# Four projection chunks of an attention layer: operations grouped into stages, PSUM banks dealt by purpose

## The chip, the cores and the metric

One core of a Trainium2 chip runs the whole program. The metric is the device time of one execution in microseconds. TensorE (PE) multiplies, ScalarE (ACT) and VectorE (DVE) work on what it leaves in PSUM, GpSimd (POOL) does small pieces, and SyncE (SP) issues most of the DMAs. PSUM has eight banks of 128 x 512 values in fp32, held here as one tensor `bank[:, 0..7, :]`.

## The reference, cut to what matters

The program computes five residual blocks over 2048 tokens of width 128: a dense mixture of experts, a state-space layer, the mixture again, a routed low-rank layer, an attention, and the low-rank layer again. The change touches the attention alone, between its normalization and its softmax:

```
q = x @ Wq; k = x @ Wk; v = x @ Wv
latent_kv = (k + v) @ W_down_kv            # 32 wide
k_rec = latent_kv @ W_up_k
v_rec = latent_kv @ W_up_v
scores = (q . k_rec) * scale               # 16 heads of 8, 2 batches of 1024
scores = clip(scores) * exp(-1e-4 * |i - j|); attn = softmax(scores)
out = (attn @ v_rec) @ Wo
```

## The kernel before, in words

The 2048 tokens are four chunks of 512 (NC = 4, CH = 512); chunks 0 and 1 are batch 0, chunks 2 and 3 are batch 1 (QC = 2). Each engine runs its own list of instructions in the order in which it was written, and semaphores tie the lists together. All that stands in `attn_rest` of each engine is the part that the change rewrites; what stands before it (the low-rank layer, ending with the normalization of chunk 3 at about 458 us) and behind it (`attn_bound`, `attn_spread`, `attn_fast`) keeps its code.

For one chunk c the projections are these steps, with the lines of the profile:

- PE `keys_values`: six matmuls of 128 x 512 (`split_matmul` twice, L1341 to L1343) add up k + v. ACT copies it to SBUF (L701, `kv_f`).
- PE `queries`: three such matmuls (L1341 to L1343). For chunks 0 and 1 DVE multiplies q with two position tables (`query_decay`, L1092, two instructions), ACT squares it (L709) and rounds the two products (`query_hi`, L717), and DVE takes the rests (`query_lo`, L1101). For chunks 2 and 3 DVE only copies q (`query_raw`, L1127), and ACT squares it.
- PE `latents`: one product with `w_down` (L1530). ACT copies it (L723, `lat_f`).
- PE `keys` (L1535) and `values_in` (L1540), both from `lat_f`. ACT squares the keys (L727) and copies the values out (`values_out`, L738). For chunks 0 and 1 DVE multiplies the keys with two tables (`key_decay`, L1107), ACT rounds (`key_hi`, L734), DVE takes the rests (`key_lo`, L1114). For chunks 2 and 3 DVE copies them (`key_raw`, L1131).
- PE `norms`: two products that sum the squares per head (L1551, L1552). DVE takes two maxima of them (`maxima`, L1121).

The rounded parts and rests go by DMA into four "stacks" (SP, L427), one per group of four heads; stack 0 of batch 0 is filled chunk by chunk, the others whole. The last `maxima` starts `attn_bound`: DVE, PE, DVE, POOL, PE and ACT in turn compute the bound that the softmax subtracts (L1179 to L1593, L794), and then the softmax's 256 exponentials run on ACT (L782) while PE computes scores (L1612) and weighted values (L1628).

Banks went by chunk: chunk c had four banks of its own, and chunk c + 2 had the same four:

```
return ((4, 5, 6, 7), (0, 1, 2, 3))[c % QC]   # q and its norms; k + v and then the values; latents and k norms; keys
```

The values of a chunk were written into the bank of k + v, so PE's `keys_values(c)` for c >= 2 waited for `v_copied`, that is for ACT's `values_out(c - 2)`.

Of the kernel before, what the change touches and what calls it, by code (L numbers as in the profile page):

```python
# [24 lines left out]
NC = T // CH  # L25
# [110 lines left out]
def build(nc, io):  # L136
    ctx = ExitStack()
    with ctx:
# [226 lines left out]
        def attn_banks(c):  # L365


            return ((4, 5, 6, 7), (0, 1, 2, 3))[c % QC]
# [9 lines left out]
        BOUND = attn_banks(QC)[3]  # L378
# [195 lines left out]
        def _(eng):  # L574
# [122 lines left out]
            def keys_values(c):  # L697
                eng.wait_ge(s["kv_ready"], c + 1)
                if c >= 2:
                    eng.wait_ge(s["lat_ready"], c - 1)  # L700
                eng.activation(kv_f(c), bank[:, attn_banks(c)[1], :], ACT.Copy).then_inc(s["kv_copied"], 1)  # L701

            def query_squares(c):
# [5 lines left out]
                eng.activation(squares(c)[0], bank[:, attn_banks(c)[0], :], ACT.Square, scale=SCALE)\  # L709
# [9 lines left out]
            def latents(c):  # L719
                eng.wait_ge(s["lat_ready"], c + 1)  # L720
                if c >= 2:
                    eng.wait_ge(s["v_ready"], c - 1)
                eng.activation(lat_f(c), bank[0:LAT, attn_banks(c)[2], :], ACT.Copy).then_inc(s["lat_copied"], 1)  # L723

            def key_squares(c):
                eng.wait_ge(s["k_ready"], c + 1)
                eng.activation(squares(c)[1], bank[:, attn_banks(c)[3], :], ACT.Square).then_inc(s["k_sq_ready"], 1)  # L727
# [8 lines left out]
            def values_out(c):  # L736
                eng.wait_ge(s["v_ready"], c + 1)
                eng.activation(values[c // QC][:, TPC * (c % QC):TPC * (c % QC + 1), :, 0:HD],  # L738
                               bank[:, attn_banks(c)[1], :].rearrange("p (t h d) -> p t h d", t=TPC, h=H), ACT.Copy)\
                   .then_inc(s["v_copied"], 1)  # L740

            def attn_first(c):
                keys_values(c)
                query_squares(c)
                query_hi(c)

            def attn_rest():
                attn_first(0)
                latents(0)
                keys_values(1)  # L750
                key_squares(0)
                key_hi(0)
                query_squares(1)
                query_hi(1)
                values_out(0)
                latents(1)
                keys_values(2)
                key_squares(1)
                key_hi(1)
                values_out(1)  # L760
                query_squares(2)
                latents(2)
                keys_values(3)
                key_squares(2)
                values_out(2)
                query_squares(3)
                latents(3)
                key_squares(3)
                values_out(3)
# [21 lines left out]
            def attention():  # L791
                attn_rest()
# [59 lines left out]
        def _(eng):  # L852
# [234 lines left out]
            def query_decay(c):  # L1087
                eng.wait_ge(s["q_ready"], c + 1)
                if c == 0:
                    eng.wait_ge(s["prep_loaded"], 16 * len(LATER))  # L1090
                for i in range(2):
                    eng.scalar_tensor_tensor(out=q_f[:, i, :], in0=bank[:, attn_banks(c)[0], :], scalar=SCALE,  # L1092
# [11 lines left out]
            def key_decay(c):  # L1104
                eng.wait_ge(s["k_sq_ready"], c + 1)
                for i in range(2):
                    eng.tensor_tensor(k_f[:, i, :], bank[:, attn_banks(c)[3], :], grow[:, i, place(c)], ALU.mult)\  # L1107
# [9 lines left out]
            def maxima(c):  # L1117
                b = c // QC
                eng.wait_ge(s["norms_ready"], c + 1)
                for i in range(2):  # L1120
                    last = eng.reduce_max(head_max[:, b, i, c % QC:c % QC + 1], bank[:, attn_banks(c)[2 * i], :],  # L1121
# [3 lines left out]
            def query_raw(c):  # L1125
                eng.wait_ge(s["q_ready"], c + 1)
                eng.tensor_copy(raw_of(q_f, c), bank[:, attn_banks(c)[0], :]).then_inc(s["q_raw"], 1)  # L1127

            def key_raw(c):
                eng.wait_ge(s["k_sq_ready"], c + 1)  # L1130
                eng.tensor_copy(raw_of(k_f, c), bank[:, attn_banks(c)[3], :]).then_inc(s["k_raw"], 1)  # L1131

            def attn_rest():
                query_decay(0)
                query_lo(0)
                key_decay(0)
                key_lo(0)
                query_decay(1)
                query_lo(1)
                maxima(0)  # L1140
                key_decay(1)
                key_lo(1)
                query_raw(2)
                maxima(1)
                key_raw(2)
                query_raw(3)
                maxima(2)
                key_raw(3)
                maxima(3)
# [188 lines left out]
        def _(pe):  # L1338
# [168 lines left out]
            def keys_values(c):  # L1507
                at, out = chunk(c), bank[:, attn_banks(c)[1], :]
# [11 lines left out]
            def queries(c):  # L1520
                at = chunk(c)
                if c >= 2:
                    pe.wait_ge(s["maxes_ready"], c - 1)
                split_matmul(bank[:, attn_banks(c)[0], :], sq_hi[:, WQ, :], sq_lo[:, WQ, :], xn_hi[:, at], xn_lo[:, at],
                             True, True).then_inc(s["q_ready"], 1)

            def latents(c):
                pe.wait_ge(s["prep_loaded"], 16 * len(LATER))
                pe.wait_ge(s["kv_copied"], c + 1)
                pe.matmul(bank[0:LAT, attn_banks(c)[2], :], w_down[:], kv_f(c), start=True, stop=True)\  # L1530
                  .then_inc(s["lat_ready"], 1)

            def keys(c):
                pe.wait_ge(s["lat_copied"], c + 1)
                pe.matmul(bank[:, attn_banks(c)[3], :], w_up[:, 0, :], lat_f(c), start=True, stop=True)\  # L1535
                  .then_inc(s["k_ready"], 1)

            def values_in(c):
                for t in range(TPC):
                    last = pe.matmul(bank[:, attn_banks(c)[1], 128 * t:128 * (t + 1)],  # L1540
# [3 lines left out]
            def norms(c):  # L1544
                pe.wait_ge(s["q_sq_ready"], c + 1)
                pe.wait_ge(s["k_sq_ready"], c + 1)
                if c >= 2:
                    pe.wait_ge(s["q_raw"], c - 1)
# [249 lines left out]
```

## Time and profile before

| | us |
|---|---|
| median of 3 runs | 824.15 |
| lowest, highest | 819.81, 825.55 |
| the profiled execution | 822.77 |
| its span, first to last instruction | 821.0 |
| PE busy, ACT busy, DVE busy, POOL busy in it | 718.6, 568.1, 497.7, 261.4 |

The span is what the trace's clock counts, 1.8 us less than the profiled execution's own time. All positions below are microseconds from the span's start. A busy PE may be a slow one: PEclk is the granted share of TensorE's full clock, 1.00 for 2.4 GHz and 0.50 for 1.2 GHz.

### The profile page before, as it was taken

To read this page: it belongs to the slowest core of one execution; us is meant where nothing else is said; L and a number is where in the kernel's file an instruction comes from. 1 tells how busy PE (TensorE), PEld (TensorE's weight loads), DVE (VectorE), ACT (ScalarE), POOL (GpSimd) and SP (SyncE) were. 2 spreads that over 40 slices of the span, in tenths; PEclk is the share of its full clock that TensorE was granted. 3 is DMA by queue.
4 is the path that set the end of the run, shared out by engine and by line. 5 is a ranking of instruction groups with operands and counts; after the bars stand their busy time and mean duration, and the time that the engine had idled before them with its cause. 6 is when DMAs were issued, how large, how long until landed. Compare 5 with 4: busy or idle time off the path is not lost.

```text
span 821.0 us, 11243 instructions
## 1 busy us (share of the span) xinstructions
PE 718.6 (88%) x3736; PEld 429.3 (52%) x3736; DVE 497.7 (61%) x1268; ACT 568.1 (69%) x800; POOL 261.4 (32%) x289
## 2 busy tenths in 40 slices
PE   2889889899898999999686696999999999999587
PEld 2567667676676777878564352323323232233364
DVE  4789878789788888888566442244423232222464
ACT  4557675667777666555344446999999999999243
POOL 2286466665666554555412000021200000000020
PEclk9999999999999999999758776999999999999958
DMA  9100000000000000000000269100079400000001
GB/s 269 42 0 2 0 1 1 0 1 2 0 1 1 0 1 2 0 1 1 0 1 0 52 127 196 36 1 1 1 134 194 85 2 1 1 1 1 3 1 51
DMA packets 14989, 24.94 MB, mean 30 GB/s; under 512 B 2720, under 2 KB 11376, under 8 KB 13424
## 3 DMA queue, kind: packets, MB, share of 16 engines
q1 hardware_dynamic: 13776, 23.79, 13.2%
q8 instruction: 31, 0.51, 0.3%
q0 software_dynamic: 224, 0.34, 0.2%
q14 instruction: 30, 0.25, 0.1%
q10 hardware_dynamic: 928, 0.06, 0.1%
HBM read 6.35 MB, written 1.05 MB: 9 GB/s over the span
## 4 chain that ended last, share of the span: by engine, by line
ACT 28%; PE 14%; issue 9%; DVE 5%; POOL 4%; ACTq 0%; POOLq 0%; DVEq 0%
ACT raw_w L782 25%; POOL act_parts L539 3%; PE bank L1341 2%; PE bank L1342 2%; PE bank L1343 2%; PE bank L1628 1%; ACT xt L609 1%; PE bank L1381 1%; PE bank L1535 1%; PE bank L1396 1%; PE bank L1612 1%; DVE xn_parts L875 1%; PE bank L1397 1%; POOL rstd L488 1%; DVE stats L865 1%
## 5 line engine op out<-in xcount | busy, mean ns | idle before, releaser
L782 ACT ACTIVATE raw_w<-bank,minus_c 128x1024 f32<-128x1024 f32 x256 | 259.3, 1161 | 4.8 <-DVE bank L1221 2.6
L539 POOL TENSOR_TENSOR act_parts<-act,act_parts 128x512 fp32r<-128x512 f32 x128 | 168.5, 1318 | 151.1 <-ACT act_parts L671 148.2
L657 ACT ACTIVATE glu<-bank,b_gate 128x512 f32<-128x512 f32 x128 | 88.1, 688 | 113.5 <-PE bank L1343 112.8
L1221 DVE TENSOR_TENSOR bank<-bank,fix 128x256 f32<-128x256 f32 x128 | 55.3, 433 | 180.4 <-PE bank L1612 180.4
L1341 PE MATMUL bank<-xn_parts,w_hi 128*128 128x512 f32 x256 | 108.0, 422 | 15.7 <-DVE up L999 8.0
L1343 PE MATMUL bank<-xn_parts,w_hi 128*128 128x512 f32 x256 | 103.0, 402 | 0.0
L1342 PE MATMUL bank<-xn_parts,w_lo 128*128 128x512 f32 x256 | 102.4, 400 | 0.0
L999 DVE TENSOR_SCALAR up<-bank,b_up 128x512 f32<-128x512 f32 x113 | 84.2, 745 | 24.7 <-PE bank L1343 24.0
L1003 DVE SCALAR_TENSOR_TENSOR bank<-glu,bank 128x512 f32<-128x512 f32 x128 | 87.9, 687 | 7.3 <-ACT glu L657 7.1
L1012 DVE SCALAR_TENSOR_TENSOR act<-up,bank 128x512 f32<-128x512 f32 x128 | 87.9, 687 | 4.4
L671 ACT ACTIVATE act_parts<-act 128x512 fp32r<-128x512 f32 x128 | 80.1, 626 | 14.8 <-DVE act L1012 14.5
L485 POOL TENSOR_SCALAR var_eps<-mean_var 128x4 f32<-128x4 f32 x28 | 7.1, 254 | 237.8 <-DVE mean_var L869 236.5
L1628 PE MATMUL bank<-raw_w 128*9 128x512 f32 x512 | 68.7, 609 | 0.0
L1628 PE MATMUL bank<-raw_w,act 128*9 128x512 f32 x512 | 68.2, 595 | 0.0
L1341 PEld LDWEIGHTS bank<-xn_parts,w_hi 128*128 128x128 f32 x256 | 49.6, 194 | 32.5 <-DVE up L999 12.3
L1463 PE MATMUL bank<-act_parts,w_hi 128*128 128x512 f32 x128 | 53.0, 414 | 4.8 <-POOL act_parts L539 4.7
L1343 PEld LDWEIGHTS bank<-xn_parts,w_hi 128*128 128x128 f32 x256 | 49.2, 192 | 11.5
L1342 PEld LDWEIGHTS bank<-xn_parts,w_lo 128*128 128x128 f32 x256 | 49.7, 194 | 9.0
L1460 PE MATMUL bank<-act_parts,w_hi 128*128 128x512 f32 x128 | 52.0, 407 | 0.4 <-ACT act_parts L671 0.4
L1448 PE MATMUL bank<-score_t,sel 128*128 128x512 f32 x128 | 51.4, 402 | 0.0
L1461 PE MATMUL bank<-act_parts,w_lo 128*128 128x512 f32 x128 | 51.4, 401 | 0.0
L609 ACT ACTIVATE xt<-bank,offset,rstd 128x128 f32<-128x128 f32 x96 | 35.9, 457 | 17.8 <-POOL offset L494 17.8
(195 smaller groups left out, 1071.2 us busy)
## 6 DMA issues: line engine op xcount, KB each, us to landing
raw_w<-in_gate_up SPq DMA_DIRECT2D x4, 512.0 KB, 9.1
w_lo<-gelu_parts SPq DMA_DIRECT2D x8, 256.0 KB, 5.4
w_lo<-act_parts SPq DMA_DIRECT2D x8, 256.0 KB, 5.5
w_hi<-gelu_parts SPq DMA_DIRECT2D x6, 256.0 KB, 4.6
w_hi<-act_parts SPq DMA_DIRECT2D x6, 256.0 KB, 5.6
x_tok<-in_x SPq DMA_DIRECT2D x4, 256.0 KB, 4.4
raw_w<-in_down SPq DMA_DIRECT2D x4, 256.0 KB, 8.5
grow<-in_grow SPq DMA_DIRECT2D x1, 1024.0 KB, 7.4
```

Of the source, the lines that this page charges most:

```text
L539: pool.tensor_tensor(act_lo[:, j % NACT, :], act[:, j % NACT, :], act_hi[:, j % NACT, :].bitcast(F32), ALU.subtract).then_inc(s["lo_ready" ...
L657: eng.activation(glu[:, j % 2, :], bank[:, G, :], ACT.Gelu_apprx_sigmoid, bias=b_gate[:, e:e + 1]).then_inc(s["glu_ready"], 1)
L671: eng.activation(act_hi[:, j % NACT, :], act[:, j % NACT, :], ACT.Copy).then_inc(s["hi_ready"], 1)
L782: eng.activation(probs[:, u % NP, :], pair, ACT.Exp, bias=minus_c[:, b:b + 1])\
L999: eng.tensor_scalar(up[:, j % 2, :], bank[:, U, :], b_up1[:, e:e + 1], 1.0 - LIMIT, ALU.add, ALU.max).then_inc(s["up_ready"], 1)
L1003: eng.scalar_tensor_tensor(out=bank[:, S[j % 2], :], in0=glu[:, j % 2, :], scalar=GLU_AT_LIMIT, in1=bank[:, S[j % 2], :], op0=ALU.min, op1 ...
L1012: eng.scalar_tensor_tensor(out=act[:, j % NACT, :], in0=up[:, j % 2, :], scalar=1.0 + LIMIT, in1=bank[:, S[j % 2], :], op0=ALU.min, op1=AL ...
L1221: eng.tensor_tensor(pair, pair, turned, ALU.mult)\
L1341: pe.matmul(out, w_hi, v_hi, start=start, stop=False)
L1342: pe.matmul(out, w_lo, v_hi, start=False, stop=False)
L1343: return pe.matmul(out, w_hi, v_lo, start=False, stop=stop)
L1628: last = pe.matmul(bank[32 * j:32 * j + VW, 6 + n % 2, :], values[b][:, kb, HG * g + j, :], probs[:, u % NP, CH * (j % 2):CH * (j % 2 + 1) ...
```

## The change

The banks are dealt by purpose: two for q (and its norms), two for k + v, one for the latents, two for the keys (and their norms), one for the values. A new function orders the operations of every engine: at each step come `norms` of the chunk three back, `keys_values` of the newest, `latents` and `queries` of the one before, `keys` and `values_in` of the one before that. DVE waits for its own rests of the chunk before (`q_lo_ready`, `k_lo_ready`) before it overwrites `q_f` or `k_f`; `norms` now waits for the keys' decay or copy too.

```diff
-        def attn_banks(c):
-            return ((4, 5, 6, 7), (0, 1, 2, 3))[c % QC]
+        Q_BANK, KV_BANK, LAT_BANK, K_BANK, V_BANK = (0, 1), (4, 5), 3, (6, 7), 2
+        def projections(kv, latents_queries, keys_and_values, norms):
+            for step in range(NC + 3):
+                for op, stage in ((norms, 3), (kv, 0), (latents_queries, 1), (keys_and_values, 2)):
+                    if 0 <= step - stage < NC:
+                        op(step - stage)
...
 # ScalarE
+            def latents_queries(c):
+                latents(c)
                 query_squares(c)
-                query_hi(c)
+                if c < QC:
+                    query_hi(c)
+            def keys_and_values(c):
+                key_squares(c)
+                if c < QC:
+                    key_hi(c)
+                values_out(c)
...
-                attn_rest()
+                projections(keys_values, latents_queries, keys_and_values, lambda c: None)
...
 # VectorE
             def query_decay(c):
                 eng.wait_ge(s["q_ready"], c + 1)
+                if c >= 1:
+                    eng.wait_ge(s["q_lo_ready"], 2 * c)
...
             def key_decay(c):
                 eng.wait_ge(s["k_sq_ready"], c + 1)
+                if c >= 1:
+                    eng.wait_ge(s["k_lo_ready"], 2 * c)
...
+            def latents_queries(c):
+                if c < QC:
+                    query_decay(c)
+                    query_lo(c)
+                else:
+                    query_raw(c)
+            def keys_and_values(c):
+                if c < QC:
+                    key_decay(c)
+                    key_lo(c)
+                else:
+                    key_raw(c)
...
-                attn_rest()
+                projections(lambda c: None, latents_queries, keys_and_values, maxima)
...
 # TensorE
             def keys_values(c):
...
-                elif c == 1:
-                    pe.wait_ge(s["xn_ready"], nth_hi(LN_ATTN, NC - 1))
-                else:
-                    pe.wait_ge(s["v_copied"], c - 1)
+                elif c >= 2:
+                    pe.wait_ge(s["kv_copied"], c - 1)
...
             def latents(c):
-                pe.wait_ge(s["prep_loaded"], 16 * len(LATER))
+                if c == 0:
+                    pe.wait_ge(s["prep_loaded"], 16 * len(LATER))
+                else:
+                    pe.wait_ge(s["lat_copied"], c)
...
             def keys(c):
                 pe.wait_ge(s["lat_copied"], c + 1)
+                if c >= 2:
+                    pe.wait_ge(s["maxes_ready"], c - 1)
...
             def values_in(c):
+                if c >= 1:
+                    pe.wait_ge(s["v_copied"], c)
...
             def norms(c):
...
+                if c < QC:
+                    pe.wait_ge(s["q_decayed"], 2 * c + 2)
+                    pe.wait_ge(s["k_decayed"], 2 * c + 2)
                 else:
-                    pe.wait_ge(s["q_decayed"], 2 * c + 2)
+                    pe.wait_ge(s["q_raw"], c - QC + 1)
+                    pe.wait_ge(s["k_raw"], c - QC + 1)
...
-                attn_rest()
+                projections(keys_values, latents_queries, keys_and_values, norms)
```

VectorE, from the first decay of the queries on, before (glu_s are the decayed queries, up the decayed keys, head_max the maxima):

```order
L1092 SCALAR_TENSOR_TENSOR glu_s<-bank,grow 128x512 x2
L1101 TENSOR_TENSOR act_parts<-glu_s,gelu_parts 128x512 x2
L1107 TENSOR_TENSOR up<-bank,grow 128x512 x2
L1114 TENSOR_TENSOR xn_parts<-up,early 128x512 x2
L1092 SCALAR_TENSOR_TENSOR glu_s<-bank,grow 128x512 x2
L1101 TENSOR_TENSOR act_parts<-glu_s,gelu_parts 128x512 x2
L1121 TENSOR_REDUCE head_max<-bank 128x1 x2
L1107 TENSOR_TENSOR up<-bank,grow 128x512 x2
```

VectorE at the same place, now (the lines of the new file lie some ten lower):

```order
L1082 SCALAR_TENSOR_TENSOR glu_s<-bank,grow 128x512 x2
L1091 TENSOR_TENSOR act_parts<-glu_s,gelu_parts 128x512 x2
L1082 SCALAR_TENSOR_TENSOR glu_s<-bank,grow 128x512 x2
L1091 TENSOR_TENSOR act_parts<-glu_s,gelu_parts 128x512 x2
L1099 TENSOR_TENSOR up<-bank,grow 128x512 x2
L1106 TENSOR_TENSOR xn_parts<-up,early 128x512 x2
L1113 TENSOR_REDUCE head_max<-bank 128x1 x2
L1120 COPY glu_s<-bank 128x512
L1099 TENSOR_TENSOR up<-bank,grow 128x512 x2
```

The queries of chunk 1 have moved ahead of the keys of chunk 0, and so has everything that waits for VectorE's decay of those keys moved behind them.

TensorE, from the keys of chunk 0 to the keys of chunk 1, before (w_up are keys and values, w_down the latents, same_head the norms, three rows with sq_hi, sq_lo, sq_hi one product of q or half of one of k + v):

```order
L1535 MATMUL bank<-tmp,w_up 128x512
L1540 MATMUL bank<-w_up,tmp 128x128 x4
L1341 MATMUL bank<-xn_parts,sq_hi 128x512
L1342 MATMUL bank<-xn_parts,sq_lo 128x512
L1343 MATMUL bank<-xn_parts,sq_hi 128x512
L1530 MATMUL bank<-glu,w_down 32x512
L1551 MATMUL bank<-score_t,same_head 128x512
L1552 MATMUL bank<-score_t,same_head 128x512
L1341 MATMUL bank<-xn_parts,sq_hi 128x512
```

TensorE from the keys of chunk 0 on, now:

```order
L1530 MATMUL bank<-tmp,w_up 128x512
L1537 MATMUL bank<-w_up,tmp 128x128 x4
L1550 MATMUL bank<-score_t,same_head 128x512
L1551 MATMUL bank<-score_t,same_head 128x512
L1331 MATMUL bank<-xn_parts,sq_hi 128x512
L1332 MATMUL bank<-xn_parts,sq_lo 128x512
```

The queries and latents of chunk 1 have gone to the front of this piece, with k + v of chunk 2 ahead of them; the norms of chunk 0 come straight behind the values of chunk 0, and k + v of chunk 3 behind the norms.

## Rows read from the trace of the kernel before

**Rows 1.** Stretches of the span: busy us of each engine (instructions), granted clock, DMA.

```profile
core 0: us, PE busy (x) PEld busy (x) DVE busy (x) ACT busy (x) POOL busy (x), PEclk, DMA share, GB/s
...
456.30:498.55 42.25, 32.53 (x98) 18.04 (x97) 20.22 (x36) 16.44 (x30) 0.71 (x1) 0.74 0.55 116
498.55:772.00 273.45, 256.91 (x1813) 84.08 (x1814) 84.20 (x200) 261.69 (x260) 11.93 (x8) 0.98 0.23 45
```

**Rows 2.** The chain of waits at the end of the projections: start us, us, what.

```profile
492.87 1.30 DVE head_max L1121 x2
...
498.55 0.85 PE bank L1612 x3
```

**Rows 3.** The same view of stretches, the projections cut where the granted clock changes.

```profile
456.30:460.40 4.10, 4.10 (x11) 2.78 (x9) 1.02 (x3) 1.19 (x2) 0.00 (x0) 0.50 0.00 0
460.40:470.64 10.24, 7.20 (x26) 3.44 (x25) 6.37 (x10) 4.79 (x9) 0.00 (x0) 1.00 0.35 82
470.64:484.30 13.66, 11.85 (x26) 6.79 (x27) 6.30 (x11) 6.22 (x12) 0.00 (x0) 0.50 0.44 101
484.30:494.20 9.90, 8.22 (x34) 4.44 (x32) 5.32 (x10) 4.06 (x7) 0.00 (x0) 1.00 0.97 177
...
498.55:508.20 9.65, 8.19 (x44) 2.67 (x48) 1.63 (x4) 7.03 (x7) 0.00 (x0) 0.50 0.98 190
```

**Rows 4.** Timeline around TensorE's gap: start us, us, engine, line, operation.

```profile
472.45 0.76 PE L1341 MATMUL bank<-xn_parts,sq_hi 128*128 128x512 f32 x1 [3.90 <-ACT raw_w L738]
```

**Rows 5.** Timeline, TensorE at 2.4 GHz.

```profile
462.43 0.39 PE L1342 MATMUL bank<-xn_parts,sq_lo 128*128 128x512 f32 x1
462.66 0.40 PE L1343 MATMUL bank<-xn_parts,sq_hi 128*128 128x512 f32 x1
464.01 1.12 PE L1535 MATMUL bank<-tmp,w_up 32*128 32x512 f32 x2 [0.95 <-ACT tmp L723]
464.97 1.05 PE L1540 MATMUL bank<-w_up,tmp 32*128 32x128 f32 x8
...
465.95 0.51 PE L1341 MATMUL bank<-xn_parts,sq_hi 128*128 128x512 f32 x1
...
466.85 1.04 PE L1530 MATMUL bank<-glu,w_down 128*32 128x512 f32 x2
467.83 0.50 PE L1551 MATMUL bank<-score_t,same_head 128*128 128x512 f32 x1
```

**Rows 6.** Timeline, TensorE at 1.2 GHz.

```profile
459.44 0.63 PE L1342 MATMUL bank<-xn_parts,sq_lo 128*128 128x512 f32 x1
...
459.86 0.63 PE L1343 MATMUL bank<-xn_parts,sq_hi 128*128 128x512 f32 x1
...
475.28 2.07 PE L1535 MATMUL bank<-tmp,w_up 32*128 32x512 f32 x2
...
477.15 1.91 PE L1540 MATMUL bank<-w_up,tmp 32*128 32x128 f32 x8
478.99 0.80 PE L1341 MATMUL bank<-xn_parts,sq_hi 128*128 128x512 f32 x1
...
480.57 1.92 PE L1530 MATMUL bank<-glu,w_down 128*32 128x512 f32 x2
```

**Rows 7.** Timeline, the first queries between VectorE and ScalarE.

```profile
460.53 1.29 DVE L1092 SCALAR_TENSOR_TENSOR glu_s<-bank,grow 128x512 f32<-128x512 f32 x2 [2.04 <-PE bank L1343]
...
461.85 0.60 ACT L709 ACTIVATE score_t<-bank 128x512 fp32r<-128x512 f32 x1 [2.01 <-DVE glu_s L1092]
...
462.34 1.14 ACT L717 ACTIVATE gelu_parts<-glu_s 128x512 fp32r<-128x512 f32 x2
...
463.07 1.29 DVE L1101 TENSOR_TENSOR act_parts<-glu_s,gelu_parts 128x512 fp32r<-128x512 f32 x2 [1.25 <-ACT gelu_parts L717]
```

**Rows 8.** Timeline, SyncE's issue of the last rests of stack 0.

```profile
481.30 1.26 SPq L427 DMA_DIRECT2D w_hi<-xn_parts  x2
```

**Rows 9.** The page of DMA issues, 440 to 620: issues, KB each, median us to landing.

```profile
w_hi<-xn_parts SPq DMA_DIRECT2D x4, 128.0 KB, 2.6
```

More of the change, by code:

```diff
@@ L376, in out_bank @@
             return 4 + c
-        BOUND = attn_banks(QC)[3]
+        BOUND = K_BANK[1]
         UNITS = G4 * QC * KB * 2
@@ L700, in keys_values @@
                     eng.wait_ge(s["lat_ready"], c - 1)
-                eng.activation(kv_f(c), bank[:, attn_banks(c)[1], :], ACT.Copy).then_inc(s["kv_copied"], 1)
+                eng.activation(kv_f(c), bank[:, KV_BANK[c % 2], :], ACT.Copy).then_inc(s["kv_copied"], 1)
             def query_squares(c):
@@ L708, in query_squares @@
                     eng.wait_ge(s["q_decayed"], 2 * c + 2)
-                eng.activation(squares(c)[0], bank[:, attn_banks(c)[0], :], ACT.Square, scale=SCALE)\
+                eng.activation(squares(c)[0], bank[:, Q_BANK[c % 2], :], ACT.Square, scale=SCALE)\
                    .then_inc(s["q_sq_ready"], 1)
@@ L722, in latents @@
                     eng.wait_ge(s["v_ready"], c - 1)
[L723 removed]
+                eng.activation(lat_f(c), bank[0:LAT, LAT_BANK, :], ACT.Copy).then_inc(s["lat_copied"], 1)
             def key_squares(c):
                 eng.wait_ge(s["k_ready"], c + 1)
[L727 removed]
+                eng.activation(squares(c)[1], bank[:, K_BANK[c % 2], :], ACT.Square).then_inc(s["k_sq_ready"], 1)
             def key_hi(c):
@@ L738, in values_out @@
                 eng.activation(values[c // QC][:, TPC * (c % QC):TPC * (c % QC + 1), :, 0:HD],
-                               bank[:, attn_banks(c)[1], :].rearrange("p (t h d) -> p t h d", t=TPC, h=H), ACT.Copy)\
+                               bank[:, V_BANK, :].rearrange("p (t h d) -> p t h d", t=TPC, h=H), ACT.Copy)\
                    .then_inc(s["v_copied"], 1)
-            def attn_first(c):
-                keys_values(c)
+            def latents_queries(c):
+                latents(c)
                 query_squares(c)
-                query_hi(c)
[L747 to L769, printed above, removed]
+                if c < QC:
[5 more added lines that the diff above has]
+                values_out(c)
             def attn_fast():
@@ L1091, in query_decay @@
                 for i in range(2):
-                    eng.scalar_tensor_tensor(out=q_f[:, i, :], in0=bank[:, attn_banks(c)[0], :], scalar=SCALE,
+                    eng.scalar_tensor_tensor(out=q_f[:, i, :], in0=bank[:, Q_BANK[c % 2], :], scalar=SCALE,
                                              in1=grow[:, 1 - i, place(c)], op0=ALU.mult, op1=ALU.mult)\
@@ L1120, in maxima @@
                 for i in range(2):
-                    last = eng.reduce_max(head_max[:, b, i, c % QC:c % QC + 1], bank[:, attn_banks(c)[2 * i], :],
+                    last = eng.reduce_max(head_max[:, b, i, c % QC:c % QC + 1], bank[:, (Q_BANK, K_BANK)[i][c % 2], :],
                                           axis=AX.X)
@@ L1507, in keys_values @@
             def keys_values(c):
-                at, out = chunk(c), bank[:, attn_banks(c)[1], :]
+                at, out = chunk(c), bank[:, KV_BANK[c % 2], :]
                 pe.wait_ge(s["xn_ready"], nth_hi(LN_ATTN, c))
@@ L1534, in keys @@
                 pe.wait_ge(s["lat_copied"], c + 1)
-                pe.matmul(bank[:, attn_banks(c)[3], :], w_up[:, 0, :], lat_f(c), start=True, stop=True)\
+                if c >= 2:
+                    pe.wait_ge(s["maxes_ready"], c - 1)
+                pe.matmul(bank[:, K_BANK[c % 2], :], w_up[:, 0, :], lat_f(c), start=True, stop=True)\
                   .then_inc(s["k_ready"], 1)
             def values_in(c):
+                if c >= 1:
+                    pe.wait_ge(s["v_copied"], c)
                 for t in range(TPC):
-                    last = pe.matmul(bank[:, attn_banks(c)[1], 128 * t:128 * (t + 1)],
+                    last = pe.matmul(bank[:, V_BANK, 128 * t:128 * (t + 1)],
                                      lat_f(c)[:, 128 * t:128 * (t + 1)], w_up[:, 1, :], start=True, stop=True)
```

70 lines of the change are left out of this document (18 added, 52 removed).

## The prediction

> **What bounds the kernel now.** I read three views in this order: the stretches of the span, the chain of waits behind the projections, and the timeline of the projections. The stretches [rows 1] set the ceiling: the projections take 456.30 to 498.55, 42.25 us of 821.0, and behind them ACT is busy 261.69 of 273.45 us with the exponentials. So the softmax is bound by ACT, and whatever the projections end earlier or later moves its start, and with it the end of the program, one for one. Ahead of 456.30 nothing is touched. What sets the end of the projections is the last pair of maxima on DVE, 492.87 to 494.16, and from there a serial chain through five engines runs to 498.55, 5.68 us after the pair's start [rows 2]. That chain keeps its code and its cost. The question is only when the last maxima start.
>
> Cut where the granted clock changes [rows 3], PE is busy 4.10 of 4.10, 7.20 of 10.24, 11.85 of 13.66 and 8.22 of 9.90 us: at 1.2 GHz it is nearly full and is the bound, at 2.4 GHz it waits for the others. The one large hole is 3.90 us before k + v of chunk 2 at 472.45, released by the copy of chunk 0's values on ACT (L738, `values_out`) [rows 4]. That is the bank wait that the change takes away. After this hole the clock was at 1.2 GHz from 470.64 to 484.30, so the hole costs more than its own length.
>
> **The prices of a step.** At 2.4 GHz a 128x512 matmul follows the one before after 0.23 us and its result is there 0.40 after its start; keys take 0.96, values 0.98, latents 0.98, and the q product with its restart 0.90, without a wait 0.70 [rows 5]. At 1.2 GHz the step is 0.43 (result after 0.63), keys 1.87, values 1.84, latents 1.85 (estimated like them, since it issues as many columns at 2.4 GHz in 0.98 as values do), q 1.28 without a wait and 1.58 with its restart [rows 6]. Norms are two steps with a restart, about 0.7 and 1.1 (estimated from the steps). On DVE a pair takes 1.29; ACT's square is 0.60 and lets the next start after 0.49; the rounding pair takes 1.14, and DVE's rests start 0.73 after ACT's first rounding [rows 7]. A handover costs 0.03 to 0.04 (460.49, when q was there, to 460.53) [rows 6, 7].
>
> **What the change removes, adds and moves, walked through with the clock as traced** (1.2 GHz to 460.4, 2.4 to 470.6, 1.2 to 484.3, 2.4 behind). No instruction is added or removed; all the work of the engines stays.
>
> Chunk 1's k + v now goes ahead of the queries: it runs 458.87 to 461.05, latents of chunk 0 to 462.02, queries of chunk 0 are ready at 462.89. Before they were ready at 460.49 [rows 6]: DVE's chain starts 2.4 us later. PE goes on with k + v of chunk 2 (462.72), latents and queries of chunk 1, keys and values of chunk 0, without a hole to 467.7: the removed wait does go away here. Then come the norms of chunk 0, which now also wait for the keys' decay. On DVE that decay stands behind both chunks' queries: decay of q0 462.92 to 464.22, ACT's square and first rounding to 465.34, rests to 466.67; decay of q1 466.69 to 468.00 (queued behind its new wait for the rests, about 0.1 each), ACT to 469.12, rests to 470.44; decay of k0 to 471.67. Two rounds of 1.30 + 1.14 + 1.30 and a pair of 1.30 stand between q0 and the norms. The norms start at 471.69, so PE is idle 3.98 us where it was idle 3.90: the hole keeps its place and length and gets another cause. Queued behind these norms on PE are k + v of chunk 3, latents and queries of chunk 2 and the keys of chunk 1, so everybody waits.
>
> From there PE is at 1.2 GHz and full: norms to 472.81, k + v 3 to 475.38, latents 2 to 477.23, queries 2 to 478.52, keys 1 to 480.38, values 1 to 482.2. Norms 1 wait for the decay of k1, 482.54, a hole of 0.35, and run 482.57 to 483.69. Latents 3 run to 485.2, queries 3 wait for the maxima of chunk 1 and run 485.24 to 486.04, keys 2 to 487.00, values 2 to 487.98; norms 2 wait for the copy of k2, 488.80 (a hole of 0.82), keys 3 489.48, values 3 to 491.4, norms 3 wait for the copy of k3, 491.98 (0.56), and end at 492.79. The last maxima run 492.82 to 494.11.
>
> The same bookkeeping with the old order ends at 493.47 (the trace has 494.16, so it is 0.7 us short). Like against like the new order is 0.6 us later, and the 4.4 us behind it stay.
>
> **The unknown: which clock goes with the new order.** Where a span falls at which level is not in my hands, so I bound it by running both orders at the same levels. At 2.4 GHz from 460.4 on: new 490.2, old 488.3, +1.9. At 1.2 GHz throughout: 501.6 against 500.6, +1.0. At 1.2 GHz from 470.6 on: 497.8 against 499.0, -1.3. The order alone is thus worth -1.3 to +1.9. The clock itself can differ between the two: against the traced level of before (493.5), the new order ends at 490.2 if the hole doesn't cost the clock, -3.2, and at 497.8 if the clock doesn't come back at 484, +4.3. In the new order the last third has more holes on PE (0.35, 0.14, 0.82, 0.56), so the upper side is likelier. I take +2.0, nearest to the row of equal clocks (+0.6) with less than half of the way to +4.3.
>
> On such holes the rows show: a gap of 0.95 us ahead of the keys of chunk 0 at 464.01 [rows 5] left the clock at 2.4 GHz, the gap of 3.90 us did not [rows 3, 4]. The Trainium skill, page "TensorE: Matmul & The Clock Gate", section "A second HAM failure mode: psum-queue depth-cycling", speaks against this change: a kernel that goes round PSUM banks leaves TensorE so many small idle spots between groups of matmuls that its clock swings between the two levels. By that rule the last third here would go at 1.2 GHz; by the row of the 0.95 us gap it would not. It is rival two below.
>
> **Covers.** SP fills stack 0 when the rests of k1 are there: before it issued them at 481.30 [rows 8]; now they come at 483.9, and with 1.26 for the two issues [rows 8] and 2.6 to landing [rows 9] they are in by some 488, over 10 us ahead of 498.55. So the later rests cost nothing; without that cover they would cost the 2.6 us. Stacks 1 to 3 shift by the same 2.6 us, and the first is read only after a quarter of batch 0's 128 exponentials. ACT has 16.44 us of work in 42.25 [rows 1], so its new order hides. DVE's two new waits for its own rests cost 0.1 each and are in the walk. PE's new waits for `lat_copied`, `v_copied` and `maxes_ready` end before PE is there, except queries 3 (0.14).
>
> **The sum.** Profiled execution 822.8 + 2.0 = 824.8. It lies 1.4 below the median of the three runs; against that the sum would be 826.2. I forecast 825.5, between the two. A measurement of this kernel tells about 1% (8.2 us) from no change, and this is far below.
>
> **The rivals.**
>
> One, the forecast: the hole stays, with the keys' decay as its cause; 823 to 826.5. Chance 0.50.
>
> Two, the clock is lost in the last third too: 822.8 + 4.3 = 827.1. For it: more small holes, work of chunk 3 spread thin. Against it: the old order had holes there too (8.22 busy of 9.90 [rows 3]) and kept 2.4 GHz. Chance 0.20.
>
> Three, the pipeline does what it is built for: PE's hole is short enough, or falls such that the clock stays at 2.4 GHz from 460.4 on: 822.8 - 3.2 = 819.6. For it: PE has five operations queued over the first part of DVE's work. Against: DVE's chain from q0 to the norms is 8.8 us, PE's queue behind q0 5.0 us, and that leaves four. Chance 0.12.
>
> Four, on the slower side: the clock never rises to 2.4 GHz at 460.4. The place is PE between k + v of chunk 1 and the norms of chunk 0; once at 1.2 GHz the whole stretch is bound by PE and ends at 501.6, +8.1, and the softmax's start at 1.2 GHz, where ACT was busy 7.03 of 9.65 us [rows 3] against 96% later [rows 1], costs some 2.2 us more if it lasts as long again: 833.1. It decides from a granted clock of 0.5 between 461 and 470. Against it: PE is as full there as before (no hole from 456.3 to 467.7). Chance 0.08.
>
> Five, the change moves nothing at the start of the softmax, since orders and waits offset each other (the -1.3 to +0.6 of equal clocks): 822.8, as before. Chance 0.10.
>
> **How the numbers follow.** The likeliest is one, 825.5. The range reaches from case three (819.6) to above case two, and leaves out most of four: 819.5 to 830. Over 1% faster only with a clock better than anywhere traced, 0.03; over 1% slower is case four, 0.08; the rest, 0.89, is within 1%.
>
> **What would show it right or wrong.** Right: the norms of chunk 0 start within 0.1 us of the end of the keys' decay of chunk 0 and after a PE gap of 3 to 5 us; k + v of chunk 2 run without a wait at about 463; the last maxima start 1 to 4 us later than 492.87, counted from k + v of chunk 0; the 5.68 us from them to the first scores unchanged. Wrong: a PE gap under 2 us before the norms of chunk 0 (then three), a first score held by a stack rather than by the bound, or a change of more than 2 us anywhere ahead of 456 or behind 499.

## The result, and the profile after

The changed kernel runs in 823.76 us (median of 20 runs, 820.91 to 829.39); the kernel before, run beside it, in 821.5 (20 runs, 815.68 to 825.92). The ratio on record is 1.0045 with a 95% interval of 1.0025 to 1.0066: some 3.7 us slower, a small loss that is clear of no change and within 1%. It is not the quotient of the two medians, which lie 2.3 us apart (1.0028, inside the interval). The profiled execution has a span of 823.4 us against 821.0.

First the stretches of the changed kernel's trace, cut where its granted clock changes (columns as in [rows 1]). The fifth row is the last third of the projections, the last two are the whole projections and the softmax:

```profile
453.88:459.20 5.32, 5.32 (x14) 3.79 (x12) 1.02 (x3) 1.19 (x2) 0.00 (x0) 0.50 0.01 3
459.20:469.45 10.25, 7.21 (x27) 3.70 (x26) 5.66 (x9) 5.88 (x11) 0.00 (x0) 1.00 0.22 52
469.45:476.28 6.83, 5.99 (x11) 3.13 (x12) 3.19 (x6) 2.61 (x5) 0.00 (x0) 0.50 0.48 116
476.28:479.70 3.42, 2.63 (x13) 1.55 (x12) 1.48 (x3) 1.39 (x4) 0.00 (x0) 1.00 0.29 75
479.70:496.00 16.30, 14.33 (x31) 7.40 (x31) 7.64 (x12) 5.26 (x9) 0.00 (x0) 0.50 0.81 153
...
453.88:500.81 46.93, 36.65 (x98) 20.17 (x97) 20.21 (x36) 16.50 (x30) 0.72 (x1) 0.65 0.52 110
500.81:774.20 273.39, 257.10 (x1814) 84.08 (x1814) 84.30 (x200) 261.68 (x260) 11.92 (x8) 0.98 0.22 44
```

The projections take 46.93 us, k + v of chunk 0 to the first scores, where they took 42.25; the softmax behind them is as long as it was (273.39 against 273.45 us, ACT busy 261.68 against 261.69) [rows 1]. TensorE's work is the same in matmuls, but its busy time rose from 32.53 to 36.65, since more of it ran at 1.2 GHz: the mean clock of the stretch is 0.65 instead of 0.74.

The timeline shows where TensorE waited and when the last maxima came. The first number in brackets is how long the engine had been idle before the row, and behind the arrow stands what released it; such idle time of TensorE is called a **hole** below:

```profile
453.88 0.78 PE L1331 MATMUL bank<-xn_parts,sq_hi 128*128 128x512 f32 x1
...
461.06 0.39 PE L1331 MATMUL bank<-xn_parts,sq_hi 128*128 128x512 f32 x1
...
468.87 1.28 DVE L1099 TENSOR_TENSOR up<-bank,grow 128x512 f32<-128x512 f32 x2
...
470.29 0.77 PE L1550 MATMUL bank<-score_t,same_head 128*128 128x512 f32 x1 [3.88 <-DVE up L1099]
...
480.35 0.77 PE L1550 MATMUL bank<-score_t,same_head 128*128 128x512 f32 x1 [1.43 <-DVE up L1099]
...
494.72 1.29 DVE L1113 TENSOR_REDUCE head_max<-bank 128x1 f32<-128x512 f32 x2 [1.54 <-PE bank L1551]
...
500.81 1.22 PE L1593 MATMUL bank<-w_hi 32*128 32x512 f32 x6 [1.89 <-issue]
```

The row at 461.06 is k + v of chunk 2, without a wait: the bank wait that held it for 3.90 us [rows 4] is gone. The row at 470.29 has taken its place: the norms of chunk 0 wait 3.88 us for the keys' decay (L1099, the old L1107), which DVE starts at 468.87 behind both chunks' queries. Norms of chunk 1 wait 1.43 us for the same operation of chunk 1.

From here on **stretch** means the time from the first matmul of k + v of chunk 0 to the start of the last pair of maxima: 492.87 - 456.30 = 36.57 us before, 494.72 - 453.88 = 40.84 after, +4.27. (Where DVE's maxima of two chunks run together, I count back 1.32 us from the operation behind them, as in before's 494.19 - 492.87.) The bound's chain behind it took 6.09 instead of 5.68 us. Against these +4.7 stands that k + v of chunk 0 started 2.42 us earlier, in code that the change doesn't touch. -2.42 + 4.27 + 0.41 and some 0.1 of rest make the 2.4 us between the spans.

Where in the stretch the 4.27 us arise, a cut at the norms of chunk 1 shows. They start 482.41 - 456.30 = 26.11 us behind k + v of chunk 0 in the trace of before and 480.35 - 453.88 = 26.47 us in the changed kernel's: up to there the two are level, holes of 3.90 and 3.88 us included, though the changed kernel has done k + v of chunk 3 by then (at a mean granted clock of 0.76 against 0.70). From there to the last maxima, before and then after:

```profile
482.41:492.87 10.46, 10.11 (x38) 5.96 (x37) 4.66 (x8) 4.64 (x8) 0.00 (x0) 0.91 0.98 184
```

```profile
480.35:494.72 14.37, 14.33 (x31) 7.37 (x31) 5.86 (x10) 4.61 (x8) 0.00 (x0) 0.50 0.84 160
```

So 3.91 of the 4.27 us lie behind the norms of chunk 1. The changed kernel has seven matmuls fewer left there, but does them all at 1.2 GHz, TensorE busy for 14.33 of 14.37 us, where before had a granted clock of 0.91. The level fell at 479.70, in the hole of 1.43 us ahead of the norms of chunk 1, which the old order doesn't have. These are two single executions. For every execution the mean granted clock of the whole span is on record: its median is 0.927 over the 20 runs of the changed kernel and 0.931 over the 35 runs of before that stand beside the first experiments.

### The profile page after: what moved, and what is told of

The parts are those of the page before. It is cut to its first block, busy times and chain, and to the rows that moved or that the text cites. A ratio compares the mean times of both kernels' runs of the same rounds, so it can differ in the third digit from the quotient of the medians.

```text
span 823.4 us, 11254 instructions
## 1 busy us (share of the span) xinstructions
PE 722.0 (88%) x3736; PEld 430.4 (52%) x3736; DVE 497.3 (60%) x1268; ACT 568.2 (69%) x800; POOL 261.3 (32%) x289
## 4 chain that ended last, share of the span: by engine, by line
ACT 27%; PE 15%; issue 9%; DVE 5%; POOL 4%; ACTq 0%; POOLq 0%; DVEq 0%
ACT raw_w L770 25%; POOL act_parts L544 3%; PE bank L1331 2%; PE bank L1333 2%; PE bank L1332 2%; PE bank L1609 1%; ACT xt L614 1%; PE bank L1371 1%; PE bank L1386 1%; PE bank L1387 1%; PE bank L1593 1%; PE bank L1523 1%; DVE xn_parts L863 1%; POOL rstd L493 1%; DVE stats L853 0%
```

## The experiments

All ratios are against the kernel before, run on the same chip, with the 95% interval. Next to the time stands the stretch of each run's one trace. The trace is one execution and its clock levels vary: in these kernels, the same ahead of the projections, k + v of chunk 0 started anywhere from 452.99 to 459.67 us. So the time's interval decides and the stretch explains. In the filled kernel before, below, the traced execution took 823.34 us with a stretch of only 31.6, and the median of its runs was 817.74.

The kernel before had a median of 821.9 us (35 runs) beside the first comparison of the banks alone, the keys ahead of queries in the first and third form, and the changed kernel filled; 819.91 (29 runs) beside the second form, before filled, the first comparison of the decays first and the second of the banks alone; and 821.59 (16 runs) beside the rest. The quotient of the medians lies inside the interval each time, but not always near the ratio; gains in microseconds go by the ratio where the medians are not named.

**The banks alone (two comparisons).** The new banks with their waits, but `projections` replaced on all three engines by the old lists (on ACT with `attn_first` written out):

```diff
-                projections(keys_values, latents_queries, keys_and_values, norms)
+                keys_values(0)
+                queries(0)
+                latents(0)
+                keys_values(1)
+                keys(0)
+                values_in(0)
...
+                norms(3)
```

Expected:

> The new banks and their waits with the old order on all three engines. Stretch means: from the first matmul of k + v of chunk 0 to the start of the last pair of maxima, 36.6 us in the trace of before and 40.8 in that of the changed kernel. Theory A (the loss is the new order: on VectorE the queries of chunk 1 stand ahead of the keys' decay of chunk 0, for which the norms of chunk 0 wait): the hole of 3.9 us before k + v of chunk 2 closes, the stretch is 33 to 36 us, and the time 1 to 3 us below before. Rival B (the loss is the dealing of the banks with its waits between TensorE and the others): stretch 38 to 41, time 1 to 3 us above before. Rival C (only the clock's levels fell otherwise, by chance): stretch 36 to 38, no difference.

> The new banks with the old order once more, since its first comparison was 0.9957 to 1.0015 and its trace had a stretch of 30.8 us. Theory A: stretch 30 to 35 and a time 1 to 4 us below before; taken together with the first, clear of no change. If the banks alone are worth nothing: ratio 1.000 within 0.2%.

Measured: 818.42 us, ratio 0.9986 (0.9957 to 1.0015), stretch 30.7; then 817.61, ratio 0.9967 (0.9935 to 0.9999), stretch 33.7. Both stretches are shorter than before's 36.57, and theory A's direction holds, though only the second interval stays, barely, below 1 (in the first the medians lie 3.5 us apart, the ratio says 1.1). The holes don't close as expected: before the keys of chunk 1 TensorE waits 1.34 us in the first trace and 2.88 us in the second, for ACT's copy of the latents (L728), and behind the 2.88 the clock falls to 0.50 for 6.83 us. What is clear is the comparison with the changed kernel: its 1.0025 to 1.0066 doesn't overlap either. With the new banks the old order costs nothing, the new order does. The rival that blamed the banks, and the one that saw chance alone, fall. The order alone on the old banks can't be tried: it puts k + v of chunk 2 ahead of the values of chunk 0, and with the old banks that would wait for them forever. So banks and order aren't fully parted: the norms wait for the keys' decay only since the new banks put the keys' norms into the keys' bank (before they went into the latents' bank), and the order makes that wait long. The new order with the norms of the keys in a bank of their own was not run.

**Keys ahead of queries, in three forms.** First on all engines:

```diff
-                for op, stage in ((norms, 3), (kv, 0), (latents_queries, 1), (keys_and_values, 2)):
+                for op, stage in ((norms, 3), (kv, 0), (keys_and_values, 2), (latents_queries, 1)):
```

> The changed kernel with keys_and_values ahead of latents_queries within a step, on all engines. Theory A: the keys of chunk 0 are decayed ahead of the queries of chunk 1, the norms of chunk 0 start without a hole of 3.9 us, the stretch is 33 to 36 us, the time 1 to 3 us below before (4 to 6 below the changed kernel). Rival B (banks and their waits): stretch 39 to 41 as in the changed kernel. Rival C (chance): the stretch keeps a hole of about 4 us and ends between 36 and 41.

Measured: 822.54 us, ratio 1.0012 (0.9986 to 1.0038), stretch 33.3. The hole before the norms of chunk 0 is down to 0.24 us, but others appear later, the largest of them 1.67 us (timeline, TensorE):

```profile
470.81 0.47 PE L1550 MATMUL bank<-score_t,same_head 128*128 128x512 f32 x1 [0.24 <-DVE up L1099]
...
477.47 0.79 PE L1331 MATMUL bank<-xn_parts,sq_hi 128*128 128x512 f32 x1 [1.67 <-DVE head_max L1113]
```

The queries of chunk 2 now wait for maxima that stand behind other work on DVE. The stretch and the closed hole are as theory A has them; the gain is about half of what I wrote (2.7 us from the changed kernel's ratio to this one's, with overlapping intervals, not 4 to 6, and nothing measurable against before, where I had written 1 to 3).

Then with `keys_and_values` first of all:

```diff
+                for op, stage in ((keys_and_values, 2), (norms, 3), (kv, 0), (latents_queries, 1)):
```

> The changed kernel with keys_and_values first in a step, then norms, keys_values, latents_queries. Theory A: the stretch is 31 to 35 us, since TensorE's norms of chunk 0 find the keys' decay done; time 1 to 4 us below before. Rival B (banks and their waits cost): 38 to 41.

Measured: 819.5 us, ratio 0.9991 (0.9962 to 1.002), stretch 32.4. Its interval lies below the changed kernel's, but a gain over before (I had written 1 to 4 us) is not shown.

Last with TensorE's order left as changed, and only ACT and DVE taking the keys first, by a flag that their two calls set:

```diff
+                ops = [(norms, 3), (kv, 0), (latents_queries, 1), (keys_and_values, 2)]
+                if late_queries:
+                    ops = [ops[0], ops[1], ops[3], ops[2]]
+                for op, stage in ops:
```

> As the changed kernel on TensorE, but ScalarE and VectorE take keys_and_values ahead of latents_queries. Theory A with VectorE's list alone as the cause: the hole before the norms of chunk 0 shrinks to under 1 us, and the stretch is near 37. If TensorE's list matters too (the keys of chunk 0 still stand behind the queries of chunk 1, and the rests of the queries now wait behind them): hole gone but new ones ahead of the queries' consumers, stretch 38 to 40, time 0 to 2 us below the changed kernel. Rival B: no change, 40 to 41.

Measured: 824.71 us, ratio 1.0039 (1.0009 to 1.007), stretch 37.5. The hole shrinks from 3.88 to 1.21 us, and a new one of 2.08 us comes up before the queries of chunk 2:

```profile
468.22 0.48 PE L1553 MATMUL bank<-score_t,same_head 128*128 128x512 f32 x1 [1.21 <-DVE up L1102]
...
474.88 0.50 PE L1334 MATMUL bank<-xn_parts,sq_hi 128*128 128x512 f32 x1 [2.08 <-DVE head_max L1116]
```

The stretch lies between the two that I had written, near 37 for ACT's and DVE's lists alone and 38 to 40 if TensorE's matters too. So these two lists alone aren't enough; the lists have to fit each other. The time is not measurably below the changed kernel's.

**The holes filled.** What a hole costs by itself and what by the clock behind it: 16 matmuls, whose result nobody reads, go into it. In the changed kernel:

```diff
             def norms(c):
+                if c == 0:
+                    for _ in range(16):
+                        pe.matmul(bank[:, KV_BANK[1], :], sq_hi[:, WK, :], xn_hi[:, chunk(3)], start=True, stop=True)
```

> The changed kernel with 16 extra matmuls of 128x512 (their result is never read) on TensorE ahead of the norms of chunk 0, where it was idle for 3.9 us: 16 x 0.23 = 3.7 us at 2.4 GHz. Theory A says that the hole costs mainly the clock: the level stays at 2.4 GHz behind it, the stretch falls from 40.8 to 33 to 35 us, the time by 4 to 7 us although work was added. If the hole's cost is its own length and the queue order alone, the stretch stays at 40 to 41 and the time at that of the changed kernel or above.

In the kernel before:

```diff
             def keys_values(c):
                 at, out = chunk(c), bank[:, attn_banks(c)[1], :]
+                if c == 2:
+                    for _ in range(16):
+                        pe.matmul(bank[:, attn_banks(1)[1], :], sq_hi[:, WK, :], xn_hi[:, chunk(3)], start=True, stop=True)
```

> The kernel before with the same 16 extra matmuls on TensorE ahead of k + v of chunk 2, where it was idle for 3.9 us. If the hole costs the clock (theory A's second half): the stretch falls from 36.6 to 31 to 33 us, at 2.4 GHz throughout, and is 2 us shorter than in the filled changed kernel (35.0), which is what the order alone costs. If the levels have nothing to do with the hole: 36 to 37.

Measured: the changed kernel filled 821.3 us, ratio 1.001 (0.9975 to 1.0044), stretch 35.0; before filled 817.74, ratio 0.997 (0.9934 to 1.0005), stretch 31.6. Timeline of TensorE in the filled changed kernel:

```profile
466.36 3.96 PE L1544 MATMUL bank<-xn_parts,sq_hi 128*128 128x512 f32 x16
470.32 0.47 PE L1553 MATMUL bank<-score_t,same_head 128*128 128x512 f32 x1
...
470.86 0.39 PE L1331 MATMUL bank<-xn_parts,sq_hi 128*128 128x512 f32 x1
...
477.65 0.47 PE L1553 MATMUL bank<-score_t,same_head 128*128 128x512 f32 x1 [1.43 <-DVE up L1099]
...
478.43 1.92 PE L1523 MATMUL bank<-glu,w_down 128*32 128x512 f32 x2
```

The norms of chunk 0 now run at 2.4 GHz, and k + v of chunk 3 behind them takes 0.23 us a step where it took 0.43. The stretch fell by 5.8 us though 16 matmuls were added, but not all of that is the filling: in this trace the clock rose to 1.00 already 2.3 us behind the start of k + v of chunk 0, in the unfilled one 5.3 us behind it, and the norms start 15.00 us behind it instead of 16.41. From the norms of chunk 0 to the last maxima it is 20.03 instead of 24.43 us, 4.4 less: that is what the clock behind the hole costs here. In the kernel before the part ahead of the hole is level: k + v of chunk 2 starts 16.16 us behind k + v of chunk 0 (16.15 unfilled), and from there the last maxima come after 15.48 instead of 20.42 us, 4.9 less. The level then falls around the hole of 1.43 us before the norms of chunk 1 (latents 1.92 for two at 478.43), the same hole at which the unfilled kernel lost it. The time of the changed kernel fell by less than I wrote (2.9 us by the ratios, and the intervals overlap), and for before filled the interval just includes no change. With both holes of 3.9 us filled the new order stays 3.4 us of stretch behind the old one, where I had written 2: so this hole is not what sets the two orders apart. The filled changed kernel still lost the clock twice (0.50 from 478.05 to 481.46 and from 484.87 on), the filled before kept 1.00 from 464.68 to 491.98.

**The decays first: a version that beats both.** The new banks, with lists written by hand. DVE decays queries and keys of a chunk before it takes the rests of either:

```diff
 # VectorE
-                projections(lambda c: None, latents_queries, keys_and_values, maxima)
+                query_decay(0)
+                key_decay(0)
+                query_lo(0)
+                query_decay(1)
+                key_lo(0)
+                key_decay(1)
+                maxima(0)
+                key_lo(1)
+                query_lo(1)
+                query_raw(2)
+                maxima(1)
+                key_raw(2)
+                query_raw(3)
+                key_raw(3)
+                maxima(2)
+                maxima(3)
```

TensorE's list, in short names (kv, lat for latents, q, k, v, norm, with the chunk): kv0 kv1 lat0 q0 k0 v0 q1 lat1 kv2 k1 norm0 v1 kv3 lat2 q2 norm1 k2 v2 lat3 q3 k3 norm2 v3 norm3. ScalarE's (ks, qs the squares, kh, qh the roundings, vo the values out): kv0 lat0 kv1 ks0 qh0 qs0 vo0 lat1 kh0 ks1 qh1 kv2 kh1 qs1 lat2 vo1 kv3 ks2 qs2 vo2 lat3 ks3 qs3 vo3.

> The new banks with lists written by hand: VectorE decays queries and keys of a chunk before it takes the rests of either (decay q0, decay k0, rests q0, decay q1, rests k0, decay k1, maxima 0, rests k1, rests q1), so ScalarE's rounding is never waited for, and TensorE has the norms of chunk 0 behind the keys of chunk 1. Theory A in full (what counts is how early VectorE's decays free TensorE): no hole over 1.5 us on TensorE, clock at 2.4 GHz from some 460 to 490, stretch 25 to 29 us, time 5 to 9 us below before. If TensorE's own work at the granted clock is the bound instead: stretch not under 31.

> The hand-written lists with the new banks once more (the first comparison was 0.985 to 0.993, its trace had a stretch of 25.4 us). If that is the kernel and not the luck of its runs: stretch 25 to 29 us, ratio 0.987 to 0.993.

Measured: 812.04 us, ratio 0.9887 (0.9847 to 0.9927), stretch 25.4; again 814.27, ratio 0.9883 (0.984 to 0.9925), stretch 26.2. The stretches are as expected. The time is 9.3 and 9.6 us less by the ratios, 7.9 and 7.3 by the medians, against the 5 to 9 that I had written. The second run's stretches of two microseconds, the first and the last of those from the middle of the projections to their end (those between have TensorE busy 2.00 each, at 1.00):

```profile
462.00:464.00 2.00, 2.00 (x12) 1.38 (x11) 1.61 (x3) 1.17 (x3) 0.00 (x0) 1.00 0.00 0
...
480.00:482.00 2.00, 1.16 (x7) 0.60 (x5) 2.00 (x5) 0.60 (x1) 0.00 (x0) 1.00 0.95 184
```

TensorE is busy without a hole, at 2.4 GHz, to the end. Against the kernel before that is 10 to 11 us less stretch and 7 to 10 us less time. All three engines' lists changed at once, so these runs don't say which of the moves matters.

**The same lists on the old banks.** The kernel before, with the lists of the decays first as far as its banks let them, and DVE's new waits for its own rests. TensorE: kv0 q0 lat0 kv1 k0 v0 q1 lat1 kv2 k1 norm0 v1 kv3 q2 lat2 norm1 k2 v2 q3 lat3 k3 norm2 v3 norm3; ScalarE: kv0 lat0 kv1 ks0 qs0 vo0 qh0 lat1 kh0 ks1 qh1 kv2 kh1 vo1 qs1 kv3 lat2 qs2 ks2 vo2 qs3 lat3 ks3 vo3; VectorE as above.

```diff
             def query_decay(c):
                 eng.wait_ge(s["q_ready"], c + 1)
+                if c >= 1:
+                    eng.wait_ge(s["q_lo_ready"], 2 * c)
...
```

> The same lists on the old banks (chunk by chunk), as far as these let them: queries ahead of latents on TensorE, ScalarE's copies of the values earlier, since k + v of chunk 2 waits for the copy of chunk 0's values and k + v of chunk 3 for that of chunk 1's. If the order of VectorE's list is nearly all of the gain (theory A): stretch 26 to 30 us, time 4 to 8 us below before. If the gain needs the new banks: stretch 31 to 36, time 0 to 4 below before.

Measured: 818.51 us, ratio 0.9947 (0.9917 to 0.9976), stretch 31.0. The old wait is back:

```profile
473.70 0.47 PE L1349 MATMUL bank<-xn_parts,sq_hi 128*128 128x512 f32 x1 [2.08 <-ACT raw_w L738]
```

So reordering on the old banks gives about half of the gain, and the new banks with the lists that go with them the other half: the stretches differ by 4.7 us and the ratios by 0.6%, though the intervals still overlap by a little (0.9917 against 0.9925). The split isn't clean, since TensorE's and ScalarE's lists are not the same in the two (here the queries go ahead of the latents and of k + v of chunk 1). Theory A's claim that the order is nearly all of it is not borne out.

**The clock for the softmax's start.** On top of the decays first: 7, 5 and 6 unread matmuls where TensorE idles in the bound's chain.

```diff
             def attn_bound():
+                for _ in range(7):
+                    pe.matmul(bank[:, KV_BANK[0], :], sq_hi[:, WK, :], xn_hi[:, chunk(3)], start=True, stop=True)
                 pe.wait_ge(s["tops_ready"], 1)
...
```

> The hand-written lists with the new banks, and extra matmuls of 128x512 (never read) where TensorE idles behind the projections: 7 ahead of the wait for the maxima, 5 ahead of the wait for the bound, 6 behind it. The first 9.65 us of the softmax ran at 1.2 GHz in before, with ScalarE busy 7.03. If the idle spots of the bound's chain cost the clock there: the granted clock is 1.00 at the softmax's start, its first 10 us have ScalarE busy over 8.5, and the time is 1 to 3 us below the same kernel without them. If the extra matmuls only stand in the way of the chain: the chain grows by their overhang, up to 1 us, and the time is the same or 1 us more.

Measured: 811.34 us, ratio 0.9845 (0.9804 to 0.9885), the lowest ratio of all, but its interval overlaps that of the kernel without the extra matmuls (0.984 to 0.9925). The first 9.65 us of the softmax, with them and without:

```profile
489.95:499.60 9.65, 7.84 (x46) 2.35 (x48) 1.91 (x5) 7.33 (x7) 0.00 (x0) 0.65 0.93 195
```

```profile
487.96:497.61 9.65, 8.19 (x48) 2.46 (x48) 1.95 (x5) 7.08 (x7) 0.00 (x0) 0.55 1.00 200
```

The clock was at 1.00 when the scores started and fell to 0.50 2.4 us later: ACT is busy 7.33 instead of 7.08, not the 8.5 that I had written. The bound's chain did not grow: 5.8 us from the last maxima to the first scores, against 6.4 and 6.7 in the two traces without. A gain in time is not shown.

## Why the prediction was right, point by point

- **The frame held.** The softmax's start moves the end one for one; nothing behind it changed (273.39 against 273.45 us), and 16.5 us of ACT work hid in the new order.
- **The removed wait and its successor held.** k + v of chunk 2 without a wait (461.06, 7.2 us behind k + v of chunk 0, forecast 6.4); the norms of chunk 0 released by the keys' decay after 3.88 us, forecast 3.98, and 0.14 us behind its end, where I had written within 0.1. The norms of chunk 1 come 26.47 us behind k + v of chunk 0, forecast 482.57 - 456.30 = 26.27. That the holes are equally long also means that this exchange is not the loss: the loss comes behind it. The banks alone show that it takes the new order.
- **The sum held, the walk in the last third did not.** Forecast was +2.0 against the profiled execution; the 20 runs say +3.7 (2 to 5.4) by the ratio and +2.3 by the medians. The forecast's walk takes 492.82 - 482.57 = 10.25 us from the norms of chunk 1 to the last maxima, with the clock back at 2.4 GHz at 484.3. The trace takes 14.37, since the level falls at 479.70 and stays at 1.2 GHz to the end. I had allowed for that by less than half of the way to +4.3, the price of rival two (the clock lost in the last third).
- **Rival two had the level right and not the reason.** Its "more small holes" (0.14, 0.82 and 0.56 us behind the norms of chunk 1) are not there: at 1.2 GHz TensorE was full. Its walk was at 1.2 GHz from 470.6 on, while the trace had 3.42 us at 2.4 GHz from 476.28. That the stretch grew by 4.27, so near to 4.3, is in part luck. By the time of the 20 runs the forecast's own case (823 to 826.5) came true, and the traced execution, 825.18 us at a mean clock of 0.923, is among the lower clocks of the 20 (0.921 to 0.934). How many of them lost the clock in the last third is not on record.
- **The absolute level** came out 1.7 us under mine. I had set 825.5 between the profiled execution's 822.8 + 2.0 and the median's 824.15 + 2.0, and the runs of before beside it had a median of 821.5.
- **The signs that I named.** The last maxima came 4.3 us later in the stretch, outside my 1 to 4. The chain behind them grew by 0.4, not 0, all in TensorE's wait that the profile puts down to nothing (1.89 before the first scores, 1.48 before). And 2.4 us were gained ahead of the stretch, where I had written that more than 2 would prove me wrong. What fell is the yardstick, not the theory: with the same code there the start moved over 6.7 us among the traces. No stack held the first score: the last pieces of stack 0 were issued at 482.19, over 18 us ahead of it.
- **The page's rule.** In the changed kernel's trace the clock does swing, up at 459.20, down at 469.45, up at 476.28, down at 479.70. So far the Trainium skill's rule on small idle spots ("TensorE: Matmul & The Clock Gate", section "A second HAM failure mode: psum-queue depth-cycling") agrees, though the two falls go with holes of 3.88 and 1.43 us and not with small spots, and the trace of before, on the old banks, swings too. The page speaks of a swing, not of a level that stays, so my reading of it for the last third went beyond it. Going round the banks alone doesn't do it: the decays first go round the same banks, and the second trace of them is at 2.4 GHz in every piece from 460 to 482. What differs is the order and with it the holes. But the length of a hole does not decide either. In the first trace of the banks alone the level, up since 455.3, fell although no hole since was longer than 0.83 us (0.52 and 0.62 of the full clock in the pieces from 462 to 466) and then stayed at 1.00 behind a hole of 1.34 us; in the second it stayed behind 0.95 us, as in my row.
- **What stays open** is why the level didn't come back in the last third. In before it rose 11.8 us behind the end of the hole of 3.90 us, in the changed kernel 6.0 us behind that of 3.88 us, and behind the hole of 1.43 us not within the 14.37 us in which TensorE was busy for 14.33. No run tests this.

## What to carry to other kernels

When a wait is removed, look in each engine's list for what now stands ahead of the operation that the next consumer needs: here a bank wait of 3.9 us became a queue wait of 3.9 us, because both chunks' queries went ahead of the first chunk's keys. The best version here put first what frees another engine (the decays, which release a bank and the norms) and later what nobody waits for soon (the rests), and let other work stand between two operations of which the second needs another engine's answer to the first; which of these did it was not tested apart. A hole can cost more than its length through TensorE's clock behind it, and filling it with unread matmuls is a quick test of how much. Compare such traces from the hole on, since the clock ahead of it differs from one execution to the next.

## What the runs showed of the hardware that I had not expected

- Sixteen added matmuls went with a stretch 5 to 6 us shorter in both kernels (40.8 to 35.0, 36.6 to 31.6), 4.4 and 4.9 us of it behind the filled hole. In time neither gain is clear of the noise.
- TensorE's clock stayed at 1.2 GHz over 14.4 us in which TensorE was busy but for 0.04 us (480.35 to 494.72 in the changed kernel), and fell at 462.1 in the first trace of the banks alone, where it had risen at 455.3 and no hole since was over 0.83 us.
- The wait before the first scores for which the profile shows no releaser is 1.48 us in the trace of before, 1.89 in that of the changed kernel, and 2.15 and 2.54 in the two of the decays first. It isn't stack 0: its last pieces were issued at 476.52 in the second of these and the scores started at 487.96. With six unread matmuls in it (the last experiment) 0.40 us of it are left idle. What it is stays open; no run tests it.
- Single executions of one kernel differ by up to 13.6 us (before, 815.07 to 828.69 over 35 runs), more than any effect here. The intervals reach 0.2% either way with 20 runs of each kernel, about 0.3% with 10 or 12 runs of the variant and 0.4% with 6.
